# One block of sixteen target tiles, from counts times features to gathered rows times one-hots

## The reference

```
h = relu(layernorm(x));  f = h
repeat 10 times:
    f   = f * src_norm[:, None]
    agg = segment_sum(f[src], dst, num_segments=12500)
    f   = 0.9 * (agg * dst_norm[:, None]) + 0.1 * h
x = x + f
```

## Time and profile before

| what | us |
|---|---|
| median of three runs | 6389.11 |
| lowest and highest run | 6384.84, 6390.48 |
| span of the profiled execution | 7018.8 |
| of it, the ten steps | 3003 to 6993 |
| TensorE, VectorE, GpSimd busy in the span | 5576.3, 4279.1, 1693.3 |

### The profile page before, as it was taken

The page is one execution under the profiler, slowest core; times in us unless marked ns, Lnnn a source line. Parts: engine busy times, 40 slices in busy tenths (PEclk is TensorE's granted clock), DMA queues, the critical chain, the costliest instruction groups (busy, mean ns, idle before and its releaser), DMA issues. The chain is left out here.

```text
span 7018.8 us, 211605 instructions
## 1 busy us (share of the span) xinstructions
PE 5576.3 (79%) x85008; PEld 3590.0 (51%) x85008; DVE 4279.1 (61%) x12668; ACT 721.3 (10%) x1695; POOL 1693.3 (24%) x1739
## 2 busy tenths in 40 slices
PE   1455555555555556589999999999999999999998
PEld 1344444444444445446565554656555565656564
DVE  7455555555555557766666666666656666666665
ACT  0122222222222223000000000000000000000000
POOL 5655555555555552500000000000000000000000
PEclk9867676666667767799999999999999999999999
DMA  4322222222222222155545555555555555555554
GB/s 117 77 75 76 76 76 77 75 76 77 79 72 79 72 76 94 27 205 194 200 183 204 192 198 205 189 200 191 201 191 201 191 201 201 189 203 189 197 197 169
DMA packets 442864, 1016.61 MB, mean 145 GB/s; under 512 B 253162, under 2 KB 371914, under 8 KB 387354
## 3 DMA queue, kind: packets, MB, share of 16 engines
q1 hardware_dynamic: 386938, 968.76, 39.0%
q0 software_dynamic: 54944, 33.96, 2.6%
HBM read 838.78 MB, written 176.58 MB: 145 GB/s over the span
## 5 line engine op out<-in xcount | busy, mean ns | idle before, releaser
L1864 PE MATMUL banks_fast<-count_units_fast,feature_parts_fast 128*32 128x512 fp8e3 x70608 | 3826.3, 379 | 31.6 <-DVE count_units_fast L1759 26.9
L1864 PEld LDWEIGHTS banks_fast<-count_units_fast,feature_parts_fast 128*32 128x32 bf16 x70608 | 2146.2, 97 | 1688.5 <-issue 37.5
L1758 DVE TENSOR_SCALAR count_units_fast<-packed_ring_fast 128x512 int32<-128x512 int32 x2949 | 1255.8, 426 | 1429.1 <-PE banks_fast L1864 1398.2
L144 POOL DMA_INDIRECT rows_fast<-row_table,idx_fast x1456 | 1408.5, 967 | 996.9 <-ACT count_stage_fast L1257 563.4
L1759 DVE TENSOR_SCALAR count_units_fast<-packed_ring_fast 128x512 int32<-128x512 int32 x2949 | 1237.2, 420 | 0.0
L1351 PE MATMUL banks_fast<-w1a_b1a_fast,turn_fast 49*128 49x96 f32 x3136 | 374.6, 375 | 810.6 <-ACT turn_fast L1262 589.6
L1223 DVE TENSOR_SCALAR window_place_hot_fast<-iota_wide_fast,local_keys_fast,target_weight_fast 128x196 bf16<-128x196 f16 x3136 | 933.9, 343 | 0.0
L1316 PE MATMUL banks_fast<-window_place_hot_fast,window_src_hot_fast 128*128 128x196 bf16 x3136 | 697.4, 312 | 115.4 <-issue 71.0
L1322 PE MATMUL banks_fast<-window_place_hot_fast,window_src_hot_fast 128*128 128x196 bf16 x3136 | 680.2, 305 | 106.1 <-issue 105.4
L1351 PEld LDWEIGHTS banks_fast<-w1a_b1a_fast,turn_fast 49*128 49x128 f32 x3136 | 294.9, 260 | 917.4 <-issue 497.4
L1316 PEld LDWEIGHTS banks_fast<-window_place_hot_fast,window_src_hot_fast 128*128 128x128 bf16 x3136 | 410.1, 155 | 224.2 <-issue 148.3
(11 more groups left out here) (282 smaller groups left out, 1551.5 us busy)
## 6 DMA issues: line engine op xcount, KB each, us to landing
packed_ring_fast<-edge_counts SPq DMA_DIRECT2D x422, 1792.0 KB, 7.0
edge_counts<-count_stage_fast SPq DMA_DIRECT2D x100, 784.0 KB
running_sums<-run_sums_fast SPq DMA_DIRECT2D x100, 768.0 KB
rows_fast<-row_table,idx_fast POOLq DMA_INDIRECT x1456
rows_fast<-attrs_padded SPq DMA_DIRECT2D x98, 128.0 KB
attrs_padded<-in_edge_attr SPq DMA_DIRECT2D x1, 12500.0 KB
rows_fast<-row_table,src_ends_fast POOLq DMA_INDIRECT x112
row_table<-h_nodes_fast SPq DMA_DIRECT2D x1, 1568.0 KB, 5.2
```

What stands on the lines that cost most here:

```text
L144: pool.indirect_dma_start(out=self.rows[:, r, c, 0:DN], out_offset=None, in_=b.dram.table, in_offset=bass.IndirectOffsetOnAxis(ap=idx[:, c ...
L1758: nc.vector.tensor_scalar(to[..., 0:P // 8], of, NIBBLES, None, ALU.bitwise_and)
L1864: last = nc.tensor.matmul(b.banks[at:at + DN, SWEEP[m % 2], 0:COLS], parts[:, side, j, k * DN:(k + 1) * DN], of_strip.bitcast(FP8), start= ...
```

## The change

The last 16 target tiles are no longer a block of the sweep (`BLOCKS = 5`). Their edges are the last of the sorted list; the last 256 x 128 = 32768 edges cover them. In each step, GpSimd gathers the 96 bf16 columns of each edge's source node from a table in HBM, 128 edges to a gather, 256 gathers, four to a group, into a ring of eight groups. TensorE multiplies each block of 128 rows (stationary, 128 x 96) with a one-hot matrix of 128 edges x 128 targets (fp8 bytes, made once ahead of the steps and kept in SBUF), whose window of targets is fixed for each block; a window that straddles two banks of four tiles is two matmuls. It does so in 64 visits of one group each, placed between the units of the sweep (unit 20 to unit 244 of a step's 245). Each of the four banks is cleared by a matmul of zeros, drained by ScalarE, folded by TensorE and turned into features by VectorE, as a block is. The feature table in HBM has two sides; ScalarE's queue stores a block's, the head's or a bank's new parts as soon as they are made, and a step's first gather waits for all stores of the step before. Ahead of the steps VectorE works out the indices and the one-hots; `x`, whose place the gathered rows take, is saved to HBM and brought back at the end. If an edge falls outside its window, the flag for the general way is set. The diff, cut to its core:

```diff
-BLOCKS = J // TILES
+BLOCKS = J // TILES - 1
+GATHERS = 256
+GROUP = 4
+GSLOTS = 8
+def window_of(c):
+    centre = (N - P * FIRST_GATHERED) - ((GATHERS - c) * P - P // 2) // PER_TARGET
+    return min(max(centre - P // 2, 0), TILES * P - P)
...
+        visit_unit = lambda visit: (200 + 36 * visit + visit // 2) // 10 if visit < 36 else max((146 + 36 * visit + visit // 2) // 10, 149)
+        fold_unit = [visit_unit(v) + FOLD_BEHIND for v in bank_visit[:-1]]
+        feature_unit = [u + LEAD for u in fold_unit]
...
         @block.gpsimd
+            pool.wait_ge(idx_made, 1)
+            with pool.Fori(0, steps2) as tt:
+                for side in range(2):
+                    t = tt * 2 + side
+                    pool.wait_ge(table_stored[side], tt * (STORES * 16) + (STORES * 16 if side else 16))
+                    for g in range(STEP_GROUPS):
+                        pool.wait_ge(group_used, t * STEP_GROUPS + (g + 1))
+                        for i in range(GROUP):
+                            c = g * GROUP + i
+                            pool.indirect_dma_start(out=rows[:, g % GSLOTS, i, :], out_offset=None, in_=b.dram.feature_rows[side],
+                                                    in_offset=bass.IndirectOffsetOnAxis(ap=idx[:, c:c + 1], axis=0)).then_inc(rows_in[g % GSLOTS], 16)
         @block.scalar
+            def keep_rows(side, where):
+                act.dma_start(b.dram.feature_rows[side].rearrange("(p j) w -> p j w", j=J)[:, where, :].rearrange("p j w -> p (j w)"),
+                              parts[:, side, where, :].rearrange("p j w -> p (j w)")).then_inc(table_stored[side], 16)
+            def drain_bank(t, k):
+                act.wait_ge(group_used, t * STEP_GROUPS + (GSLOTS + (bank_visit[k] + 1) * PE_GROUPS))
+                act.wait_ge(bank_folded, t * GBANKS + (k + 1))
+                nc.scalar.copy(bank_drain[0:WF, k % 2, :], b.banks[0:WF, GATHER_BANK[k % 2], 0:BANK_COLS]).then_inc(bank_drained, 1)
...
+            act.dma_start(b.dram.x_saved, b.x[:, :]).then_inc(x_kept, 16)
+            keep_rows(0, slice(0, J))
         @block.vector
+            for c in range(0, GATHERS, PIECE):
+                nc.vector.tensor_tensor(hots[:, c:c + PIECE, :], b.iota16[:, :].unsqueeze(1).broadcast_to([P, PIECE, P]),
+                                        local16[:, c:c + PIECE].unsqueeze(2).broadcast_to([P, PIECE, P]), ALU.is_equal).then_inc(hots_made, 1)
...
         @block.tensor
+            def fold_bank(t, k):
+                pe.wait_ge(bank_drained, t * GBANKS + (k + 3))
+                for a in range(BANK_TILES):
+                    at = BANK_FOLD_AT + a * DN
+                    last = nc.tensor.matmul(b.banks[:, HEAD_FOLD, at:at + DN], bank_drain[0:WF, k % 2, a * P:(a + 1) * P], stack[0:WF, :],
+                                            start=True, stop=True)
+            def gathered_sums(t, visit):
+                for g in range(visit * PE_GROUPS, (visit + 1) * PE_GROUPS):
+                    pe.wait_ge(rows_in[g % GSLOTS], t * (STEP_GROUPS // GSLOTS * GROUP * 16) + (g // GSLOTS + 1) * (GROUP * 16))
+                    for i in range(GROUP):
+                        c = g * GROUP + i
...
+                        for lo, hi in ((w, cut), (cut, w + P)):
+                            if lo < hi:
+                                last = nc.tensor.matmul(b.banks[0:WF, GATHER_BANK[k % 2], lo - k * BANK_COLS:hi - k * BANK_COLS],
+                                                        rows[:, g % GSLOTS, i, :], hots[:, c, lo - w:hi - w].bitcast(FP8),
+                                                        start=False, stop=False, skip_group_check=True)
+                    last.then_inc(group_used, 1)
+            def sweep_and_gather(t, m, side, first, last_unit):
+                for v in range(first, last_unit):
+                    sweep_units(t, m, side, v, v + 1)
+                    at = m * BLOCK_UNITS + v
+                    for visit in range(GATHERS // per_visit):
+                        if visit_unit(visit) == at:
+                            gathered_sums(t, visit)
+                    if at in fold_unit:
+                        fold_bank(t, fold_unit.index(at))
...
             sweep_units(0, 0, 0, 0, AHEAD)
+            pe.wait_ge(hots_made, GATHERS // 32)
```

More of the change, by code:

```diff
@@ L87, in __init__ @@
         self.counts = dram("edge_counts", (CHUNKS, P, J + SLOTS, KC, P // 2), U8)
+        self.feature_rows = [dram(f"feature_rows{side}", (NP, WF), BF16) for side in range(2)]
+        self.x_saved = dram("x_saved", (P, J * DN))
 class Kept:
@@ L1734, in _ @@
+            act.dma_start(b.dram.x_saved, b.x[:, :]).then_inc(x_kept, 16)
+            keep_rows(0, slice(0, J))
             act.sem_inc(drained, 2)
             act.sem_inc(head_drained, 1)
[L1736 to L1744, removed]
+            act.sem_inc(bank_drained, 2)
@@ new lines, in _ @@
+            with act.Fori(0, steps2) as tt:
+                for side in range(2):
+                    t = tt * 2 + side
+                    drain_block(t, side, 0)
+                    keep_block(t, side, 0)
+                    drain_bank(t, 0)
+                    drain_block(t, side, 1)
+                    keep_bank(t, side, 0)
+                    keep_block(t, side, 1)
+                    drain_block(t, side, 2)
+                    drain_bank(t, 1)
+                    drain_head(t)
+                    keep_block(t, side, 2)
+                    keep_bank(t, side, 1)
+                    drain_block(t, side, 3)
+                    drain_bank(t, 2)
+                    keep_block(t, side, 3)
+                    keep_head(t, side)
+                    keep_bank(t, side, 2)
+                    drain_bank(t, 3)
+                    drain_block(t, side, 4)
+                    keep_bank(t, side, 3)
+                    keep_block(t, side, 4)
@@ L1880, in sweep_head @@
                 last.then_inc(head_swept, 1)
+            def sweep_and_gather(t, m, side, first, last_unit):
[7 more added lines that the diff above has]
+                        fold_bank(t, fold_unit.index(at))
+            pe.wait_ge(ends_made, 3 + 8)
+            for of, what in enumerate((row_f, local_f)):
+                for h in range(2):
+                    at = of * GATHERS + h * P
+                    last = nc.tensor.transpose(b.banks[:, GATHER_BANK[0], at:at + P], what[:, h * P:(h + 1) * P], b.ident[:, :])
+            last.then_inc(ends_turned, 1)
             pe.wait_ge(stacked, STRIPS + 1)
```

252 lines of the change are left out of this document (199 added, 53 removed).

## The result

The changed kernel takes 6149.27 us (median; 6147.7 to 6150.21) against 6389.8 us for the kernel before in the same session: a ratio of 0.9626 [0.9612, 0.9639], 240.5 us less. The forecast was 104 less, 6285. The sign and the mechanism came out as forecast, the size did not.

A forecast was written before the change was run, and what follows sets the result against it. TensorE's matmul columns alone were taken to bound the steps. A step: 333.4 + 41.0 + 3.8 + 1.0 + 4.5 = 383.7 us, 14.4 less; total 6389 - 144 + 36 + 4 = 6285 us, range 6115 to 6520.

The forecast's parts named there:

- What bounds the kernel: Ten propagation steps: bound by TensorE's matmul columns alone, a unit of 24 matmuls every 1.295 us, no wait hidden.
- What is left of the step, 333.4: Each step without one block of six: 398.1 - 64.7 = 333.4 us.
- A pair, 0.085: Load of 96 stationary columns and pass of 128 one-hot columns in a visit: 0.085 us, bounds 0.054 and 0.17.
- the halves: 45 of the 256 windows straddle two banks and are two matmuls: 45 x 0.085 = 3.8 us a step.
- The change of shape, 0.3: TensorE going from the sweep's strips to another shape and back: 0.3 us in each of 64 visits a step.
- case C: Visits on TensorE: cheap, 0.42 us each with pairs at the sweep's rate, step about 367, time 6113 us; chance 0.16.
- the main case: Whole kernel: 6285 us, own range 6200 to 6370 from 0.55 and 0.72 us a visit and start 23 to 40; chance 0.50.
- Clears and bank folds, 1.0 and 4.5: TensorE in each step: four bank clears 1.0 us in all, four bank folds 4.5 us in all.
- The gathers, hidden at 1.36 each: GpSimd's 256 gathers a step: 1.36 us each, chain of 365 us under the step's 383.7, hidden up to 1.43 each.
- Work costed at nothing: VectorE's changed openings and feature chains, ScalarE's stores and drains, DMA engines' loads: no added time.
- The start, 36: Ahead of the steps, VectorE's preparations and one-hots: the propagation stage's start moves by 36 us, between 23 and 40.
- The profile's excess of 630 us: The profiled span's 630 us above the median lie ahead of 3003 us, in stages the change does not touch.

The follow-up runs named there:

- a quarter of the gathers: One gather made of each group of four, all four pairs reading its rows, against the kernel after the change: 6140.12 us, ratio 0.9626.
- the doubled kernel: Every matmul of a visit issued twice, against the kernel after the change: 6293.23 us, ratio 0.9864.
- the second profile of before: The unchanged kernel before the change, run once more for its profile: 6382.37 us.
- the kernel with the later wait: TensorE's wait for one-hots moved to the first visit, units 7 and 8 opened among them, against the kernel after the change: 6137.82 us, ratio 0.9610.

## Why the prediction was wrong: point by point

- *What bounds the kernel*: right, before and after; a quarter of the gathers changes nothing that can be told, and a matmul more or less changes a visit by its own price.
- *What is left of the step, 333.4*: right. 245 units x 1.295 = 317.3, the head 8.8, the blocks' folds and the head's fold 5.8: 331.9, and 1.4 us of idle time (13.4 over 9.8 steps).
- ***A pair, 0.085*: this is the step that failed.** It measured 0.056 (0.053 on the mean of 301 matmuls). The prediction took the first stage's bf16 pair as "nearest in type, with more columns on both sides" and carried its time over unscaled. The earlier trace rows had the answer: 0.085 for 196 columns is 0.434 ns a column, at a granted clock of 1.00 there, and 128 columns at that are 0.0555. The sweep agrees at another width: a round of 512 columns takes 1.295 / 6 = 0.216, or 0.42 ns a column. So the sweep's rate was no lower bound but the value. The f32 pairs of the earlier trace rows could not be scaled like this, and why is not shown here. They cost 0.11 with 128 moving columns and 0.115 with 32, and after the change eight of 32 columns (L2054, a bank's fold) again take 3156.72 - 3155.80 = 0.92:

```profile
3155.80 1.08 PE L2054 MATMUL banks_fast<-stacked_identities_fast,x_nodes_fast 96*128 96x32 f32 x8
3156.72 1.14 PE L2030 MATMUL banks_fast<-unit_identity_fast,drained_fast 128*128 128x128 f32 x8
```

  The pairs and the halves together were put at 256 x 0.085 + 3.8 = 25.6 a step and take about 15 to 16 (the doubled kernel's 15.2, with the idle time 15.8): 10 us a step, 100 us of the missing 136.
- The Trainium skill has a rate for a stream of load and matmul pairs of 128 columns ("TensorE: Matmul & The Clock Gate", section "Back-to-back issue gap"): about 81 ns. By it the step would be 256 x (0.081 - 0.056) = 6.4 longer and the time an estimated 6213. The trace does not agree: behind the first of a visit these pairs, of 96 stationary columns, come every 0.056.
- *The change of shape, 0.3*: 0.25 by the timeline, 0.22 to 0.23 by the kernels with fewer visits. 64 x 0.05 to 0.08 is another 3 to 5 us a step. The visit as a whole, 0.47, lies between case C's 0.42 and the 0.55 where the main case's own range began, and the measured 6149 lies between C's 6113 and that range's lower edge, 6200. (Its upper edge, 6370, is not what its own terms give: 0.72 a visit and 40 at the start come to some 6350.)
- *Clears and bank folds, 1.0 and 4.5*: a fold takes 0.91 to 1.01, four 3.9.
- *The gathers, hidden at 1.36 each*: right. They come every 1.31 (334 us from a step's first to its last), the chain leaves 34 us between steps, and no visit waits. That GpSimd gets through beside VectorE's opening instructions at this price was the argument from the earlier trace rows; the turn was put at 1.43 each for a step of 383.7. By the same terms it is (369.4 - 17.1) / 256 = 1.376 for the step that came out, so the 1.36 that was chosen would only just have been hidden. The kernel with an eighth more gathers shows what lies beyond it.
- *Work costed at nothing*: right; VectorE still waits for TensorE for 1310 of its 1360 idle us, and opens in 0.443 instead of 0.426.
- *The start, 36*: 43, above the 40 of the upper bound. The one-hots took 34.8 us, about the slow rate that was chosen, and VectorE reached them 25.1 us after the stage's first load, where the working's terms add up to 21.5.
- *The profile's excess of 630 us*: right, as the second profile of before shows.

Together: -144 became -287 in the steps, +40 became +47 around them.

## What to carry to other kernels

Before carrying a matmul's time over to another shape, look for two rows of different widths. Where they agree on the time per moving column at the same clock (here 196 and 512 columns), scale by the columns. Where they agree on the time itself (here f32 pairs of 32 and 128 columns), don't. The rule ends below the widths that were compared: pairs of 40 to 88 columns cost 0.045 here, where 64 columns by the rule are 0.028. A change of shape between matmuls has a price of its own, here a quarter of a microsecond a visit, more than the four pairs inside it, so put more work into each visit until what feeds it becomes the bound. Measure how far a hidden stream is from the path by giving it more work: an eighth more gathers took the whole gain away.

## What the runs showed of the hardware that was not expected

The first gather of the stage took 34.30 us. It began beside the first of the eight one-hot instructions, which have both inputs in SBUF and start 0.08 us before the one ahead ends, and it ended 1.0 us after the last of them. In the kernel with the later wait, opening instructions stand among the eight, without a gap, and the first gather took 37.18 us. Beside the line of the first gather further up belongs VectorE's, with the first four of the eight one-hot instructions; the second line is GpSimd's in the kernel with the later wait:

```profile
2383.41 17.42 DVE L1983 TENSOR_TENSOR gathered_hots<-iota_row_fast,f_nodes_fast 128x4096 uint8<-128x4096 bf16 x4
...
2385.09 37.18 POOL L1798 DMA_INDIRECT x_nodes_fast<-feature_rows,x_nodes_fast  x1 [25.08 <-DMA feature_rows<-feature_parts_fast]
```

One more kernel told apart whether it is the kind of instruction or the missing gap:

```
                                         ...ALU.is_equal).then_inc(hots_made, 1)
+                dve.wait_ge(hots_made, c // PIECE + 1)
```

> VectorE waits for each of the eight one-hot instructions before it starts the next, at the start of the stage only; everything else is as after the change. In the trace after the change the first gather takes 34.3 us and ends with the last of the eight, which overlap each other by 0.08 us. If GpSimd's write is shut out for as long as such instructions follow each other without a gap: the first gather shall now take at most 5 us, and several more go out among the eight. If a whole chain of such instructions keeps it out whatever the gaps: still 34 us. The time changes by no more than the 8 gaps, +0.5 us, in either case: the first visit is due over 20 us after its rows.

Measured: 6145.01 us, ratio 0.9623 [0.9607, 0.9639], no change, as expected. VectorE's first three of the eight, and GpSimd's timeline beside them:

```profile
2380.40 13.33 DVE L1983 TENSOR_TENSOR gathered_hots<-iota_row_fast,f_nodes_fast 128x4096 uint8<-128x4096 bf16 x3
2381.93 3.73 POOL L1798 DMA_INDIRECT x_nodes_fast<-feature_rows,x_nodes_fast  x1 [25.03 <-DMA feature_rows<-feature_parts_fast]
2385.97 4.12 POOL L1798 DMA_INDIRECT x_nodes_fast<-feature_rows,x_nodes_fast  x1 [0.30 <-issue]
2390.40 4.15 POOL L1798 DMA_INDIRECT x_nodes_fast<-feature_rows,x_nodes_fast  x1 [0.30 <-issue]
```

Now a gather ends 0.8 to 0.9 us after each one-hot instruction, and eight go out in the time of one; the gap between two of VectorE's instructions is 0.04 us. So here a gather was shut out for as long as the chain had no gap, and a gap of 0.04 us let it in. The Trainium skill ("SBUF — State Buffer", "Who interferes with whom") says that a VectorE instruction with two SBUF inputs contends with GpSimd's reads and that a holder keeps the shared ports for the whole instruction; the runs agree, and add that without a gap the gather stays out through VectorE's next instruction too, 34.30 us over eight of them.
